# Padding mask tables of the last attention layer: built by ScalarE one phase earlier, and read by TensorE at a block address

## The chip, the cores and the metric

The kernel runs on one NeuronCore of a Trainium2 chip. A core has TensorE (matrix products), VectorE (DVE), ScalarE (ACT), GpSimd (POOL) and SyncE (SP, which issues the DMAs here), each with its own instruction stream, joined by semaphores. The metric is the device time of one execution in microseconds; the median of the executions counts.

## What is computed

The input x is 64 sequences of 64 tokens of width 256. Four transformer layers with a conditioning vector follow each other, each an attention and an MLP: layer 0 (one head, softmax then gelu MLP), layer 1 (16 heads of 16, rotary, gated MLP), layer 2 (16 heads of 64), layer 3 (16 heads of 16, with a padding mask). All is float32 in accuracy. What matters here is the mask of layer 3:

```python
attn = jnp.einsum('bhnd,bhmd->bhnm', q, k) * scale
mask = padding_mask[:, None, :] & padding_mask[:, :, None]
attn = jnp.where(mask[:, None, :, :], attn, -1000000000.0)
attn = jax.nn.softmax(attn, axis=-1)
```

## The kernel before

**Tiling.** The 4096 tokens are cut into 8 blocks of 512 (8 sequences, 4 tiles of 128 tokens). The work runs in 8 phases: attn 0, mlp 0, attn 1, mlp 1, attn 2, mlp 2, attn 3, mlp 3. In each phase the 8 blocks go through one body: block 0 is written out, blocks 1 to 6 are a hardware loop on each engine, block 7 is written out. `order_of` gives, by hand, the order of the stages in a body; every engine walks that same list and emits only its own part of each stage. `own`, `prev` and `nxt` are stages of this block, of the one before and of the one after: while a block's products run, the next one is normalised (`stats`, `norm`), transposed (`turn`), and split (`split`).

**Precision.** A float32 product is made of three products of a high and a low part (lines 541 to 543 of `project`). So every activation is split: ScalarE writes the high part (`h_hi`, line 766; `hid_hi`, line 896), VectorE subtracts it (`h_lo`, line 1030; `hid_lo`, line 1141). Those subtractions read two operands from SBUF. The weights of the next phase are split by GpSimd in eight shares, one to a block: stage `share`, `split_next`, a CAST (line 1187) and a subtraction (TENSOR_TENSOR, line 1189). SP loads the next share into `stage` when the one before it is split.

**The mlp body.** `up` k is a product of the block's 512 tokens with 128 hidden columns, into one of two score banks; ScalarE applies gelu (line 891) and the high part (line 896); VectorE makes `hid_lo`; `down` k accumulates. TensorE runs up 3, down 1, up 4, down 2, up 5, down 3, then `turn` (line 578, which transposes `xn`, the output of VectorE's `norm`, line 1010 in layers 0 and 1 and line 1012 in layers 2 and 3), up 6, down 4 and so on.

**GpSimd's part of it.** In `stats` GpSimd adds eps and takes the power (lines 1228, 1230). In block 0 of mlp 0 and of mlp 2 the stage `share` first calls `prepare_attention`, which clears the key and value tiles of the coming layer (memsets, lines 1194 to 1200). In mlp 2 it then calls `prepare_mask`: four TENSOR_SCALARs over 128x2048 (lines 1209, 1210) turn the uint8 `mask_rows` into two bf16 tables, `mask_qs` and `mask_ks`. Only then is the share of the weights split.

**The attn 3 body.** For each of 8 head groups (`scores` k), TensorE puts a mask product (line 629) into the bank before the score products (line 632). That product reads `mask_q_now` and `mask_k_now`, which hold the tiles of the current block only. The stage `mask` fills them: GpSimd copies four tiles of each table (line 1219), once for c = 0 and once for c = 1 of each block. The copy for c = 1 stands at the top of the body and waits until all scores of the block before are done (`s_full1`); the copy for c = 0 of the next block stands after `scores` 5. The stage `share` stands behind the first of them on GpSimd. In attn 1 and attn 3 GpSimd also adds the shift in `turn` (line 1235) into `hm`, from which ScalarE makes `h_hi` and VectorE `h_lo`. In VectorE's order, `scores` 4 and `back` (line 1164) stand ahead of `split` (line 1030).

Of the kernel before, what the change touches and what calls it, by code (L numbers as in the profile page):

```python
# [29 lines left out]
ALU = mybir.AluOpType  # L30
# [47 lines left out]
def order_of(kind, layer):  # L78
# [23 lines left out]
    if layer in (1, 3):  # L102
        mask = (lambda c, off: [("mask", c, off)]) if layer == 3 else (lambda c, off: [])
        return mask(1, 0) + [own("scores", 0), prev("probs_t", 7), own("q", 1), own("q_out", 1), prev("pv", 6), own("share"),
                own("scores", 1), own("probs_t", 0), own("v", 0), prev("pv", 7), own("v_out", 0), own("v", 1),
                own("v_out", 1), nxt("stats"),
                own("scores", 2), nxt("norm"), own("probs_t", 1), prev("merge"), own("k", 1), own("k_out", 1), own("pv", 0),
                own("scores", 3), own("probs_t", 2), prev("proj"), own("pv", 1), nxt("turn"),
                own("scores", 4), own("probs_t", 3), prev("back"), nxt("split"), own("pv", 2),
                own("scores", 5)] + mask(0, 1) + [own("probs_t", 4), own("pv", 3), nxt("k", 0), nxt("k_out", 0),  # L110
                own("scores", 6), own("probs_t", 5), own("pv", 4), nxt("q", 0), nxt("q_out", 0),
                own("scores", 7), own("pv", 5), own("probs_t", 6)]
# [38 lines left out]
def counts_of(kind, layer):  # L151

    c = dict(stats_raw=1, stats=1, mean_sq=1 if layer < 2 else 0, rstd_in=1, rstd=1, normed=1, eps_added=1, modded=2,
             h_hi=2, h=2, out_rows=2, x_done=1)
    if kind == "mlp":
        n = HID * (2 if layer == 1 else 1)
        c.update({"s_full0": n // 2, "s_full1": n // 2, "s_free0": n // 2, "s_free1": n // 2,
                  "hid32": HID, "hid_hi": HID, "hid": HID, "down": HID, "gate_in": HID if layer == 1 else 0,
                  "back": 1})
        return c  # L160
    n = 1 if layer == 0 else PAIRS
    c.update({"s_full0": n - n // 2, "s_full1": n // 2, "s_free0": n - n // 2, "s_free1": n // 2,
              "row_max": n, "shifted": n * (2 if layer == 0 else 1), "t_full": 0 if layer == 2 else n, "probs_t": n})
    if layer in (0, 2):
        c.update(probs=n, row_sum=n, row_inv=n, divided=n)
    if layer == 0:
        c.update(q=2, k=2, v=2, w_full=3, w_free=1, att_hi=2, att=2)
    if layer in (1, 3):
        c.update(o_full=n, o_inv=n // 2, o_free=n // 2, q=2 * 2, k=4 * 2, v=2 * 2, q32=2, w_full=3, w_free=1, att_hi=2, att=2)
    if layer == 1:  # L170
        c.update(rot_a=4, rot_b=4, k32=2)
    if layer == 3:
        c.update(mask_now=2)
    if layer == 2:
        c.update(q=n, k=n, v=8, o_full=n, o_free=n, att_hi=n, att=n, proj=n, w_full=1)
    return c
# [6 lines left out]
def build(nc, x_in, cond_in, mask_k_in, mask_q_in, vec_in, modw_in, weights_in, out, phases=len(PHASES)):  # L183
# [13 lines left out]
    with ExitStack() as ctx:  # L197
# [7 lines left out]
        w0_ready = ctx.enter_context(nc.semaphore("w0_ready"))  # L205
        t1_ready = ctx.enter_context(nc.semaphore("t1_ready"))
        mask_cleared = ctx.enter_context(nc.semaphore("mask_cleared"))
        mask_loaded = ctx.enter_context(nc.semaphore("mask_loaded"))
# [37 lines left out]
        eps_t = place("eps_t", [P, 4, TILES], F32)  # L246
        half_t = place("half_t", [P, TILES], F32)
        mx = place("mx", [P, 2, SEQ], F32)
        sm = place("sm", [P, 2, SEQ], F32)
# [34 lines left out]
        v0_sb = place("v0_sb", [P, TILES, D], F32, free + 12288)  # L284
        mask_q_now = place("mask_q_now", [P, 2, TILES, P], BF16, free3 + 4096)
        mask_k_now = place("mask_k_now", [P, 2, TILES, P], BF16, free3 + 6144)
        mask_qs = place("mask_qs", [P, tiles, 2, S], BF16, wb + 32768)
# [107 lines left out]
        def is_first(b):  # L395

            return isinstance(b, int) and b == 0
# [93 lines left out]
        def _(pe):  # L491
# [65 lines left out]
            def stage_of(ph, s, k, b):  # L557
# [42 lines left out]
                elif s == "scores":  # L600
# [23 lines left out]
                    else:  # L624
                        pe.wait_ge(sem["q"], n_at("q", ph, b, 2 * (c + 1)))
                        pe.wait_ge(sem["k"], n_at("k", ph, b, 4 * (c + 1)))
                        if layer == 3:
                            pe.wait_ge(sem["mask_now"], n_at("mask_now", ph, b, c + 1))
                            nc.tensor.matmul(dst.rearrange("p (r w) -> p r w", w=P), mask_q_now[:, c, j, :],
                                             mask_k_now[:, c, j, :].unsqueeze(1).to_broadcast([P, 4, P]), start=True, stop=False)  # L630
                        for g in range(2):
# [107 lines left out]
        def _(act):  # L739
# [7 lines left out]
            def table_part(n):  # L747
                if n == 0:
                    nc.scalar.activation(cond_silu[:, :, :], cond[:, :, :], ACT.Silu).then_inc(mod_act, 1)
                    act.wait_ge(mod_mm, 2)  # L750
                    for kc in range(DC):
                        nc.scalar.activation(t1_g[:, kc, :], psum[:, TABLE_BANKS[0], (2 + kc) * batch:(3 + kc) * batch],
                                             ACT.Silu, bias=col("t1_b", 2 + kc)).then_inc(mod_act, 1)

            def stage_of(ph, s, k, b):
                kind, layer = PHASES[ph]
                c, j, slot = k // 4, k % 4, k % 2
                if s == "table":
                    table_part(k)
                if is_first(b) and (s, k) == ("k_out", 0):  # L760
                    act.wait_ge(prepared, 4 if layer == 1 else 8)
# [146 lines left out]
        def _(dve):  # L908
# [21 lines left out]
            nc.vector.memset(half_t[:, :], -0.5).then_inc(consts_ready, 1)  # L930
            nc.vector.memset(pb[:, :, :], 0.0).then_inc(consts_ready, 1)
            full = 8 * batch
            dve.wait_ge(consts_ready, 6)
# [237 lines left out]
        def _(pool):  # L1171
# [32 lines left out]

            def prepare_mask():

                pool.wait_ge(mask_loaded, 16)
                for g in range(2):
                    nc.gpsimd.tensor_scalar(mask_qs[:, :, g, :], mask_rows[:, :, :], -MASKED, None, ALU.mult).then_inc(prepared, 1)
                    nc.gpsimd.tensor_scalar(mask_ks[:, :, g, :], mask_rows[:, :, :], 0.0, col("ident", g), ALU.is_equal, ALU.mult).then_inc(prepared, 1)  # L1210
                prepares[0] += 4
                pool.wait_ge(prepared, prepares[0])

            def mask_of_block(ph, c, b):

                pool.wait_ge(sem["s_full1"], n_at("s_full1", ph, b, -2 if c == 0 else 0))
                now = bass.ds(b * TILES, TILES)
                for dst, src in ((mask_q_now, mask_qs), (mask_k_now, mask_ks)):
                    ins = nc.gpsimd.tensor_copy(dst[:, c, :, :].rearrange("p t (g k) -> p t g k", k=S), src[:, now, :, :])
                ins.then_inc(sem["mask_now"], 1)  # L1220

            prepares = [0]
            def stage_of(ph, s, k, b):
# [19 lines left out]
                elif s == "divide":  # L1243
# [6 lines left out]
                    nc.gpsimd.tensor_tensor(ap, ap, inv, ALU.mult).then_inc(sem["divided"], 1)  # L1250
                elif s == "mask":
                    mask_of_block(ph, k, b)
                elif s == "share":
                    if is_first(b):
                        pool.wait_ge(sem["x_done"], n_at("x_done", ph, 0, 1))
                        if PHASES[ph + 1:ph + 2] in ([("attn", 1)], [("attn", 3)]):
                            prepare_attention()
                        if PHASES[ph + 1:ph + 2] == [("attn", 3)]:
                            prepare_mask()
                    split_next(ph, b)  # L1260
# [96 lines left out]
```

## Time and profile before

| | us |
|---|---|
| median of 3 runs | 2225.43 |
| lowest and highest | 2223.94 and 4509.24 |
| the profiled execution, whole | 2222.83 |
| its span from first to last instruction | 2221.0 |
| TensorE busy in that span | 2087.0 |
| VectorE busy | 1344.9 |
| ScalarE busy | 997.9 |
| GpSimd busy | 407.9 |

Busy times of different engines overlap. Of the three timed runs two lie 1.5 us apart and one stands far away.

### The profile page before, as it was taken

Reading aid. Unit: us, or ns where it says so; the run is one execution under the profiler, and the core shown is the slowest. Engines: PE = TensorE matmul, PEld = TensorE weight load, DVE = VectorE, ACT = ScalarE, POOL = GpSimd, SP = SyncE. Lnnn points to the kernel's source line nnn. Section 1 sums busy time; section 2 is a strip of 40 time slices with the busy share of each in tenths; the row PEclk is TensorE's granted clock in tenths of the full one; section 3 lists DMA queues with packets and bytes.
Section 4 is the critical chain, followed back from the end, with each engine's and each line's share of the span. In section 5 each row is a group of like instructions: output and inputs, shape, how many; then the busy total and the mean of one; then the engine's idle time right before and its main releaser. Section 6 shows DMA issues by size and latency. Waiting matters only on the chain.

```text
span 2221.0 us, 45198 instructions
## 1 busy us (share of the span) xinstructions
PE 2087.0 (94%) x15856; PEld 1692.9 (76%) x15856; DVE 1344.9 (61%) x2570; ACT 997.9 (45%) x1608; POOL 407.9 (18%) x425
## 2 busy tenths in 40 slices
PE   5889999999999999999999999998899999999998
PEld 4777788777777778787777777776688787787887
DVE  4564665667767565654555544546766677775664
ACT  2443455545444333334444444444344555554443
POOL 1121211223222010110112111112511222220000
PEclk9999999999999999999999999999999999999999
DMA  5000000000000000000000000000000000000000
GB/s 213 10 14 9 8 11 7 15 8 14 7 14 10 10 19 9 19 10 11 7 6 5 0 5 5 5 1 13 5 7 5 10 10 10 5 5 1 28 19 29
DMA packets 17855, 33.30 MB, mean 15 GB/s; under 512 B 1266, under 2 KB 11762, under 8 KB 17138
## 3 DMA queue, kind: packets, MB, share of 16 engines
q1 hardware_dynamic: 17778, 32.25, 4.5%
q8 instruction: 50, 0.82, 0.2%
q14 instruction: 27, 0.22, 0.0%
HBM read 28.06 MB, written 4.19 MB: 15 GB/s over the span
## 4 chain that ended last, share of the span: by engine, by line
PE 76%; DVE 10%; issue 8%; ACT 3%; POOL 2%; DVEq 0%; DMA 0%; ACTq 0%; SPq 0%; POOLq 0%
PE psum L541 20%; PE psum L543 19%; PE psum L542 19%; PE psum L632 4%; PE psum L645 3%; PE psum L578 2%; PE psum L665 2%; PE psum L731 2%; PE psum L679 1%; PE psum L621 1%; DVE xn L1010 1%; DVE h_lo L1030 1%; PE psum L498 1%; DVE hm L1020 1%; DVE hm L1025 1%
## 5 line engine op out<-in xcount | busy, mean ns | idle before, releaser
L541 PE MATMUL psum<-h_hi,w_lo 128*128 128x512 f32 x1152 | 479.7, 416 | 28.2 <-DVE h_lo L1030 21.6
L543 PE MATMUL psum<-h_hi,w_hi 128*128 128x512 f32 x1152 | 457.9, 398 | 0.0
L542 PE MATMUL psum<-h_lo,w_hi 128*128 128x512 f32 x1152 | 457.7, 397 | 0.0
L1141 DVE TENSOR_TENSOR hid_lo<-hid,hid_hi 128x512 fp32r<-128x512 f32 x256 | 201.7, 788 | 263.2 <-ACT hid_hi L896 262.9
L541 PEld LDWEIGHTS psum<-h_hi,w_lo 128*128 128x128 f32 x1152 | 218.8, 190 | 85.4 <-issue 25.8
L896 ACT ACTIVATE hid_hi<-hid 128x512 fp32r<-128x512 f32 x256 | 161.9, 632 | 225.7 <-PE psum L543 134.7
L543 PEld LDWEIGHTS psum<-h_hi,w_hi 128*128 128x128 f32 x1152 | 218.1, 189 | 53.8
L542 PEld LDWEIGHTS psum<-h_lo,w_hi 128*128 128x128 f32 x1152 | 218.7, 190 | 42.1
L1082 DVE TENSOR_REDUCE mx<-psum 128x8 f32<-128x512 f32 x192 | 132.4, 690 | 160.6 <-PE psum L621 107.3
L891 ACT ACTIVATE hid<-psum,vec 128x512 f32<-128x512 f32 x192 | 131.9, 687 | 199.9 <-PE psum L543 197.9
L541 PE MATMUL psum<-hid_hi,w_lo 128*128 128x512 f32 x512 | 202.8, 396 | 5.8 <-DVE hid_lo L1141 3.9
L542 PE MATMUL psum<-hid_lo,w_hi 128*128 128x512 f32 x512 | 201.1, 393 | 0.0
L543 PE MATMUL psum<-hid_hi,w_hi 128*128 128x512 f32 x512 | 200.3, 391 | 0.0
L1228 POOL TENSOR_TENSOR ms<-ms,eps_t 128x4 f32<-128x4 f32 x64 | 14.2, 222 | 895.6 <-DVE ms L1005 468.0
L1250 POOL TENSOR_TENSOR pb<-pb,ri 128x512 f32<-128x512 f32 x72 | 75.1, 1043 | 523.2 <-DVE ri L1097 523.2
L632 PE MATMUL psum<-kx,qb 128*128 128x256 f32 x512 | 136.5, 389 | 14.2 <-ACT qb L828 9.6
L645 PE MATMUL psum<-vec,pb 128*128 128x128 f32 x800 | 123.1, 277 | 24.0 <-ACTq L797 13.1
L645 PEld LDWEIGHTS psum<-vec,pb 128*128 128x128 f32 x800 | 96.8, 141 | 53.3 <-issue 24.6
L1085 DVE TENSOR_TENSOR pb<-psum,mx 128x512 f32<-128x512 f32 x192 | 132.8, 692 | 6.6
L541 PEld LDWEIGHTS psum<-hid_hi,w_lo 128*128 128x128 f32 x512 | 96.2, 188 | 30.5 <-DVE hid_lo L1141 4.9
L857 ACT ACTIVATE pt<-psum 128x512 f32<-128x512 f32 x128 | 76.2, 595 | 94.6 <-PE psum L645 89.6
L1164 DVE TENSOR_TENSOR xres<-xres,psum 128x1024 f32 (+1 forms) x64 | 78.1, 1221 | 66.6 <-PE psum L731 62.4
(118 smaller groups left out, 3717.3 us busy)
## 6 DMA issues: line engine op xcount, KB each, us to landing
stage<-in_w_dram SPq DMA_DIRECT2D x24, 256.0 KB, 2.7
stage<-in_w_dram SPq DMA_DIRECT2D x8, 512.0 KB, 3.5
out_dram<-xres SPq DMA_DIRECT2D x8, 512.0 KB, 2.9
xres<-in_x_dram SPq DMA_DIRECT2D x1, 3584.0 KB, 18.9
modw_mod<-in_modw_dram SPq DMA_DIRECT2D x2, 1536.0 KB, 13.8
stage<-in_w_dram SPq DMA_DIRECT2D x8, 384.0 KB, 3.3
stage<-in_w_dram SPq DMA_DIRECT2D x8, 192.0 KB, 2.4
modw_film<-in_modw_dram SPq DMA_DIRECT2D x1, 1024.0 KB, 6.9
```

The costliest lines, as they stand in the source:

```text
L541: nc.tensor.matmul(dst, s_lo, m_hi, start=start and j == 0, stop=False)
L542: nc.tensor.matmul(dst, s_hi, m_lo, start=False, stop=False)
L543: ins = nc.tensor.matmul(dst, s_hi, m_hi, start=False, stop=stop and j == len(pairs) - 1)
L632: ins = nc.tensor.matmul(dst.rearrange("p (r g k) -> p r g k", g=2, k=S)[:, :, g, :], qb[:, c, 2 * j + g, :, :].rearrange("p h q -> p (h q)"),
L645: ins = nc.tensor.transpose(dst[:, t * P:(t + 1) * P], pb[:, slot, t * P:(t + 1) * P], ident)
L857: nc.scalar.activation(pt[:, slot, :], probs_tp, ACT.Exp, scale=SCORE_SCALE[layer]).then_inc(sem["probs_t"], 1)
L891: nc.scalar.activation(hid32[:, slot, :], scores[slot], func, bias=col(f"u{layer}", k)).then_inc(sem["hid32"], 1)
L896: nc.scalar.activation(hid_hi[:, slot, :], hid32[:, slot, :], ACT.Copy).then_inc(sem["hid_hi"], 1)
L1082: nc.vector.tensor_reduce(top, sc, AX.X, ALU.max).then_inc(sem["row_max"], 1)
L1085: nc.vector.tensor_tensor(dst, sc, top, ALU.subtract).then_inc(sem["shifted"], 1)
L1141: nc.vector.tensor_tensor(hid_lo[:, slot, :], hid32[:, slot, :], hid_hi[:, slot, :].bitcast(F32), ALU.subtract).then_inc(sem["hid"], 1)
L1164: nc.vector.tensor_tensor(xs, xs, src, ALU.add).then_inc(sem["x_done"], 1)
```

## The change

The tables `mask_qs` and `mask_ks` are made by ScalarE. `mask_table(n)` is one ACTIVATE over 128x2048; n = 0 to 3 are issued in block 0 of mlp 2 ahead of the gelus of up 3, 4, 5 and 6. The signs of the two tables are both turned: `mask_qs` is +MASKED times the mask, and `mask_ks` is (mask times a one-hot column) minus that column, taken as the bias `no_seq`, which VectorE writes at the start of the kernel. `prepare_mask` on GpSimd is gone. The copies to `mask_q_now` and `mask_k_now`, the stage `mask`, its semaphore and TensorE's wait for it are gone. The mask product reads the tables at tile `b * TILES + j`: in the hardware loop this address comes from a register. TensorE waits once, ahead of the first mask product, for the finished tables.

```diff
 (order_of, layers 1 and 3)
-        mask = (lambda c, off: [("mask", c, off)]) if layer == 3 else (lambda c, off: [])
-        return mask(1, 0) + [own("scores", 0), prev("probs_t", 7), own("q", 1), own("q_out", 1), prev("pv", 6), own("share"),
+        return [own("scores", 0), prev("probs_t", 7), own("q", 1), own("q_out", 1), prev("pv", 6), own("share"),
...
-                own("scores", 5)] + mask(0, 1) + [own("probs_t", 4), own("pv", 3), nxt("k", 0), nxt("k_out", 0),
+                own("scores", 5), own("probs_t", 4), own("pv", 3), nxt("k", 0), nxt("k_out", 0),
 (TensorE, scores)
-                            pe.wait_ge(sem["mask_now"], n_at("mask_now", ph, b, c + 1))
-                            nc.tensor.matmul(dst.rearrange("p (r w) -> p r w", w=P), mask_q_now[:, c, j, :],
-                                             mask_k_now[:, c, j, :].unsqueeze(1).to_broadcast([P, 4, P]), start=True, stop=False)
+                            if k == 0 and is_first(b):
+                                pe.wait_ge(mask_made, 5)
+                            q_bad, k_bad = (m.rearrange("p t g k -> p t (g k)")[:, bass.ds(b * TILES + j, 1), :]
+                                            for m in (mask_qs, mask_ks))
+                            nc.tensor.matmul(dst.rearrange("p (r w) -> p r w", w=P), q_bad.rearrange("p t w -> p (t w)"),
+                                             k_bad.to_broadcast([P, 4, P]), start=True, stop=False)
 (ScalarE)
+            def mask_table(n):
+
+                g = n % 2
+                if n < 2:
+                    nc.scalar.activation(mask_qs[:, :, g, :], mask_rows[:, :, :], ACT.Copy, scale=MASKED).then_inc(mask_made, 1)
+                else:
+                    nc.scalar.activation(mask_ks[:, :, g, :], mask_rows[:, :, :], ACT.Identity, bias=no_seq[:, g:g + 1],
+                                         scale=col("ident", g)).then_inc(mask_made, 1)
+
...
+                if PHASES[ph] == ("mlp", 2) and s == "up" and 3 <= k < 7 and is_first(b):
+                    if k == 3:
+                        act.wait_ge(mask_loaded, 16)
+                        act.wait_ge(mask_made, 1)
+                        act.wait_ge(sem["x_done"], n_at("x_done", ph, 0, 1))
+                    mask_table(k - 3)
 (VectorE, start of the kernel)
+            nc.vector.tensor_scalar(no_seq[:, :], col("ident", 0, 2), -1.0, None, ALU.mult).then_inc(mask_made, 1)
 (GpSimd)
-            def prepare_mask():
-
-                pool.wait_ge(mask_loaded, 16)
-                for g in range(2):
-                    nc.gpsimd.tensor_scalar(mask_qs[:, :, g, :], mask_rows[:, :, :], -MASKED, None, ALU.mult).then_inc(prepared, 1)
-                    nc.gpsimd.tensor_scalar(mask_ks[:, :, g, :], mask_rows[:, :, :], 0.0, col("ident", g), ALU.is_equal, ALU.mult).then_inc(prepared, 1)
...
-            def mask_of_block(ph, c, b):
-
-                pool.wait_ge(sem["s_full1"], n_at("s_full1", ph, b, -2 if c == 0 else 0))
-                now = bass.ds(b * TILES, TILES)
-                for dst, src in ((mask_q_now, mask_qs), (mask_k_now, mask_ks)):
-                    ins = nc.gpsimd.tensor_copy(dst[:, c, :, :].rearrange("p t (g k) -> p t g k", k=S), src[:, now, :, :])
-                ins.then_inc(sem["mask_now"], 1)
...
-                        if PHASES[ph + 1:ph + 2] == [("attn", 3)]:
-                            prepare_mask()
```

## Rows read from the trace of the kernel before

**Rows 1.** The page: busy us by engine, and the chain's shares by engine.

```profile
PE 2087.0 (94%) x15856; PEld 1692.9 (76%) x15856; DVE 1344.9 (61%) x2570; ACT 997.9 (45%) x1608; POOL 407.9 (18%) x425
...
PE 76%; DVE 10%; issue 8%; ACT 3%; POOL 2%; DVEq 0%; DMA 0%; ACTq 0%; SPq 0%; POOLq 0%
```

**Rows 2.** Busy by window, stats to stats: block 0 of mlp 2, mlp 0, mlp 3.

```profile
core 0: us, PE busy (x) PEld busy (x) DVE busy (x) ACT busy (x) POOL busy (x), PEclk, DMA share, GB/s
1546.79:1585.92 39.13, 26.61 (x110) 21.25 (x109) 31.50 (x30) 11.06 (x17) 35.31 (x13) 0.87 0.01 4
223.99:252.47 28.48, 24.78 (x109) 20.13 (x109) 18.29 (x29) 12.20 (x20) 9.40 (x8) 0.94 0.02 7
2031.89:2055.03 23.14, 23.14 (x110) 18.94 (x109) 13.68 (x30) 10.98 (x17) 1.72 (x2) 1.00 0.01 1
```

**Rows 3.** Timeline of PE: start, us, what, [idle before <- releaser]; mlp 2, then mlp 0.

```profile
1560.21 1.97 PE L578 MATMUL psum<-vec,xn 128*128 128x128 f32 x8 [8.58 <-DVE xn L1012]
...
1572.16 0.50 PE L541 MATMUL psum<-hid_hi,w_lo 128*128 128x512 f32 x1 [3.93 <-DVE hid_lo L1141]
...
232.32 1.97 PE L578 MATMUL psum<-vec,xn 128*128 128x128 f32 x8 [3.70 <-DVE xn L1010]
```

**Rows 4.** Timeline of DVE, block 0 of mlp 2, then of mlp 0.

```profile
1548.63 11.52 DVE L1012 TENSOR_SCALAR xn<-xres,mv,rstd 128x256 f32<-128x256 f32 x4 [1.18 <-POOL rstd L1230]
...
1567.99 4.12 DVE L1141 TENSOR_TENSOR hid_lo<-hid,hid_hi 128x512 fp32r<-128x512 f32 x1
...
225.69 6.58 DVE L1010 TENSOR_SCALAR xn<-xres,rstd 128x256 f32<-128x256 f32 x4 [1.18 <-POOL rstd L1230]
232.19 2.08 DVE L1141 TENSOR_TENSOR hid_lo<-hid,hid_hi 128x512 fp32r<-128x512 f32 x2
```

**Rows 5.** Timeline of POOL, block 0 of mlp 2.

```profile
1548.54 3.52 POOL L1194 MEMSET kx<- 128x4096 f32 x1
...
1554.63 5.38 POOL L1209 TENSOR_SCALAR mask_qs<-mask_rows 128x2048 bf16<-128x2048 uint8 x1
...
1573.29 7.66 POOL L1210 TENSOR_SCALAR mask_ks<-mask_rows,vec 128x2048 bf16<-128x2048 uint8 x1
```

**Rows 6.** ACT: timeline in mlp 2, then groups by form (busy, mean ns).

```profile
1551.66 0.63 ACT L896 ACTIVATE hid_hi<-hid 128x512 fp32r<-128x512 f32 x1 [0.69 <-PE psum L543]
...
L896 ACT ACTIVATE hid_hi<-hid 128x512 fp32r<-128x512 f32 x256 | 161.9, 632 | 225.7 <-PE psum L543 134.7 <-DVE hid L1136 82.2
...
L836 ACT ACTIVATE pb<-pb 64x256 f32<-64x256 f32 x16 | 6.7, 416 | 17.4 <-DVE pb L1068 17.3
```

**Rows 7.** Timeline of POOL, one turn of attn 3's loop.

```profile
1864.99 2.04 POOL L1235 TENSOR_TENSOR hm<-hm,mod 128x512 f32<-128x512 f32 x2 [9.29 <-DVE hm L1020]
...
1876.79 0.61 POOL L1219 COPY mask_k_now<-mask_ks 128x512 bf16 x1
1877.35 0.61 POOL L1187 CAST w_hi<-stage 128x512 f32 x1
1878.13 1.28 POOL L1189 TENSOR_TENSOR w_lo<-stage,w_hi 128x512 f32 x1 [0.17 <-POOL w_hi L1187]
```

**Rows 8.** Timelines of DVE and PE, the same turn of the loop.

```profile
1868.18 1.29 DVE L1030 TENSOR_TENSOR h_lo<-hm,h_hi 128x512 fp32r<-128x512 f32 x2
...
1869.60 0.49 PE L541 MATMUL psum<-h_hi,w_lo 128*128 128x512 f32 x1 [0.91 <-DVE h_lo L1030]
```

**Rows 9.** Timelines of POOL and DVE, mlp 1: a weight split beside a two-input subtraction.

```profile
782.55 2.42 POOL L1189 TENSOR_TENSOR w_lo<-stage,w_hi 128x1024 f32 x1 [0.17 <-POOL w_hi L1187]
...
782.67 2.85 DVE L1141 TENSOR_TENSOR hid_lo<-hid,hid_hi 128x512 fp32r<-128x512 f32 x1 [0.70 <-ACT hid_hi L896]
```

**Rows 10.** Timeline of DVE, the last h_lo ahead of attn 3.

```profile
1741.59 1.98 DVE L1030 TENSOR_TENSOR h_lo<-hm,h_hi 128x512 fp32r<-128x512 f32 x2 [0.61 <-ACT h_hi L766]
```

**Rows 11.** Timeline of PE: first mask product of a loop block, then of block 7.

```profile
1877.55 0.39 PE L629 MATMUL psum<-mask_k_now,mask_q_now 128*128 128x512 bf16 x1 [0.30 <-POOL mask_k_now L1219]
...
1977.52 0.38 PE L629 MATMUL psum<-mask_k_now,mask_q_now 128*128 128x512 bf16 x1 [0.18 <-issue]
```

More of the change, by code:

```diff
@@ L171, in counts_of @@
         c.update(rot_a=4, rot_b=4, k32=2)
-    if layer == 3:
-        c.update(mask_now=2)
     if layer == 2:
@@ L206, in build @@
         t1_ready = ctx.enter_context(nc.semaphore("t1_ready"))
+        mask_made = ctx.enter_context(nc.semaphore("mask_made"))
         mask_cleared = ctx.enter_context(nc.semaphore("mask_cleared"))
@@ L247, in build @@
         half_t = place("half_t", [P, TILES], F32)
+        no_seq = place("no_seq", [P, 2], F32)
         mx = place("mx", [P, 2, SEQ], F32)
@@ L284, in build @@
         v0_sb = place("v0_sb", [P, TILES, D], F32, free + 12288)
-        mask_q_now = place("mask_q_now", [P, 2, TILES, P], BF16, free3 + 4096)
-        mask_k_now = place("mask_k_now", [P, 2, TILES, P], BF16, free3 + 6144)
         mask_qs = place("mask_qs", [P, tiles, 2, S], BF16, wb + 32768)
@@ L1203, in prepare_attention @@
                     pool.wait_ge(prepared, prepares[0])
-            def prepare_mask():
-                pool.wait_ge(mask_loaded, 16)
-                for g in range(2):
-                    nc.gpsimd.tensor_scalar(mask_qs[:, :, g, :], mask_rows[:, :, :], -MASKED, None, ALU.mult).then_inc(prepared, 1)
-                    nc.gpsimd.tensor_scalar(mask_ks[:, :, g, :], mask_rows[:, :, :], 0.0, col("ident", g), ALU.is_equal, ALU.mult).then_inc(prepared, 1)
-                prepares[0] += 4
-                pool.wait_ge(prepared, prepares[0])
-            def mask_of_block(ph, c, b):
-                pool.wait_ge(sem["s_full1"], n_at("s_full1", ph, b, -2 if c == 0 else 0))
-                now = bass.ds(b * TILES, TILES)
-                for dst, src in ((mask_q_now, mask_qs), (mask_k_now, mask_ks)):
-                    ins = nc.gpsimd.tensor_copy(dst[:, c, :, :].rearrange("p t (g k) -> p t g k", k=S), src[:, now, :, :])
-                ins.then_inc(sem["mask_now"], 1)
             prepares = [0]
@@ L1250, in stage_of @@
                     nc.gpsimd.tensor_tensor(ap, ap, inv, ALU.mult).then_inc(sem["divided"], 1)
-                elif s == "mask":
-                    mask_of_block(ph, k, b)
                 elif s == "share":
```

## The prediction

> **What bounds the kernel.** I read the page first. TensorE is busy 2087.0 of 2221.0 us and 76% of the chain that ended last is its matmuls [rows 1]. GpSimd is busy 18% of the span. So taking work off GpSimd is worth nothing by itself; it is worth something only where GpSimd makes someone late, and the sum has to be made from TensorE's idle time at the places that the change touches. Those are block 0 of mlp 2 and attn 3.
>
> Next I read the windows. From the `stats` of one block to the `stats` of the next, block 0 of mlp 2 takes 39.13 us. The same stretch of mlp 0 takes 28.48 and that of mlp 3 takes 23.14 [rows 2]. The three phases do the same number of matmuls (109 or 110) on blocks of one size. They differ in what GpSimd does: 35.31 us of work, 9.40 us, 1.72 us. mlp 3 prepares nothing, mlp 0 only clears tiles, mlp 2 clears tiles and builds the mask tables.
>
> The timeline of TensorE says where the 16 us over mlp 3 sit: it stands still 8.58 us for `xn` and 3.93 us for a `hid_lo` [rows 3]. Neither waits for GpSimd by name. But the timeline of VectorE shows the two producers stretched: four `norm` instructions take 11.52 us and one `hid_lo` 4.12 us [rows 4], while GpSimd runs without a pause from the memset at 1548.54 to the end of the last table at 1580.95 [rows 5]. In mlp 3's stretch, with 1.72 us of GpSimd, VectorE does the same list in 13.68 us instead of 31.50 [rows 2]. GpSimd's long instructions hold VectorE up, and VectorE holds TensorE up.
>
> A rule of the Trainium skill says why (SBUF — State Buffer, section Who interferes with whom): VectorE and GpSimd share one pair of SBUF ports, and a VectorE instruction in a two-port mode, or one with two SBUF inputs against a GpSimd instruction that reads SBUF, waits for the whole of the other's instruction. The stretched rows agree.
>
> **Part 1: the tables leave GpSimd in mlp 2.** Removed are four TENSOR_SCALARs, from 1554.63 to 1580.95, so 26.3 us of GpSimd [rows 5]. The memsets stay. Block 0 of mlp 0 is this case already played: the same memsets beside the same `norm`, then one share of weights. There `norm` takes 6.58 us, TensorE stands 3.70 us for it, and no second gap follows [rows 3, 4]. So I take the difference of the two windows: 39.13 - 28.48 = 10.65 us saved [rows 2]. A check by pieces: `norm` starts at 1548.63 and would end 6.58 later, at 1555.2, so `turn` starts there instead of at 1560.21, 5.0 us earlier [rows 3, 4]; the gap of 3.93 goes; together 8.9. The rest is clock: TensorE's mean granted clock in the window is 0.87 against 0.94 [rows 2]. Of 39.13 us, 13% below full is 5.1 us of lost clock, against 1.7 in mlp 0; part of that difference of 3.4 falls into idle time, the rest makes up the remaining 1.7. Both ways meet near 10.6.
>
> **Part 2: ScalarE makes them.** Four ACTIVATEs over 2048 elements. The trace has none so long. From 256 and 512 elements, 0.416 and 0.632 us, the slope is 0.84 ns an element, so one takes 0.632 + 1536 x 0.00084 = 1.93 us, an estimate; four are 7.7 us [rows 6]. ScalarE now stands idle about 0.7 us ahead of each gelu and again ahead of each high part, 1.4 us to a chunk of hidden columns [rows 6]. Three tables ahead of the high part of up 5 therefore make it 3 x (1.93 - 1.4) = 1.6 us late: it ends near 1553.9 instead of 1552.29 [rows 6]. Nobody notices: VectorE takes `hid_lo` 4 and 5 only after `norm`, that is after 1555.2, and the fourth table falls into TensorE's remaining wait of some 3.6 us. I book 0. If a table took twice as long, the high part of up 5 would be ready near 1559.6 and TensorE's down 5 would wait 1 to 2 us; that end goes into the range. `no_seq` is one tiny VectorE instruction while the input is loading: 0. TensorE's wait for the tables comes a whole phase after they are done: 0.
>
> **Part 3: the copies go from attn 3.** The copies themselves (0.61 us each, 32 of them [rows 7]) delay nothing in the loop: each set is copied well before the product that reads it, and in the loop's turn shown here `h_lo` takes its normal 1.29 [rows 8]. At the entry they do: they run beside the split of block 0's `h`, and that pair takes 1.98 us against 1.29 in the loop [rows 8, 10]. TensorE waits for it. Saved: 0.69 us, once.
>
> **Part 4: what moves into the hole.** `share` stood behind a copy that waited for the last scores of the block. So its CAST ran at 1877.35 and its subtraction at 1878.13 [rows 7], when VectorE was reading PSUM. Without that wait nothing holds it: the load of the share was issued when the one before it was split, most of a turn earlier, and GpSimd reaches it right after `turn`, whose two adds end at 1867.03 [rows 7]. CAST starts near 1866.97, the subtraction 0.78 later, at 1867.75, and it lasts 1.28 us, to 1869.03 [rows 7]. But at 1868.18 VectorE starts `h_lo`, the pair for which TensorE already waits 0.91 us in each block [rows 8]. mlp 1 shows this meeting: GpSimd's subtraction ends at 784.97 and VectorE's, started during it, at 785.52, 0.55 us behind [rows 9]. So the first `h_lo` ends at 1869.03 + 0.55 = 1869.58 and the second, 0.61 later, at 1870.19 instead of 1869.47: 0.72 us late. There is no slack, because TensorE is waiting for it, and all that follows in the block moves with it. This happens in the turns of blocks 1 to 7, seven times: 7 x 0.72 = 5.0 us lost. (For block 0's turn, where copies stretched `h_lo` too, I take the same: the subtraction is as much longer than the copy.)
>
> By the skill's rule taken literally (the same section: the whole instruction is held) `h_lo` would begin only at 1869.03 and take its full 0.69, so 0.86 late, seven times 6.0 us and a saving 1 us smaller than mine. The rule speaks against this half of the change, and agrees with the row of mlp 1 in kind.
>
> **Part 5: addresses from a register.** In the loop each mask product needs two addresses, and loses a wait. 48 products have them (8 in each of blocks 1 to 6). No matmul of the kernel before has a register address. Where the sequencer is ahead of the array this is free. At the top of the loop it is not: there the idle time before the product is 0.30 us, against 0.18 in block 7, where all values are constants [rows 11]. That difference of 0.12 pays for the few register steps with which the loop works out the values that it waits for, so two steps more and one less cost up to 0.1 us. Booked: 6 x 0.1 = 0.6. Lower end 0; upper end 0.2 at each of the 48, 9.6 us.
>
> **The sum.** -10.65 - 0.69 + 5.0 + 0.6 = -5.7 us. The span goes from 2221.0 to 2215.3, the profiled execution from 2222.83 to about 2217.1. The median of before is 2.6 above its profiled execution, so the median after is 2225.43 - 5.7 = 2219.7.
>
> **The rivals.**
> 1. *The weight split does not collide* (GpSimd reaches it later, or VectorE gets in first). For it: the two start only 0.43 us apart. Against it: their order follows from one event, VectorE's `hm`. Then parts 1, 3 and 5 stand alone: -10.7, time 2214.7.
> 2. *Slower: the register addresses are paid at every product.* The gain without them is 6.3 us; over 48 products it is gone from 0.13 us each on. With 0.2 us each it is +9.6 - 6.3 = +3.3, time 2228.7. Against it: in the loop only the first product of a block has such idle time before it.
> 3. *ScalarE is late*: a table takes far more than 1.9 us, or the function with a bias and a column scale reloads its table. Costs 2 to 3 us: 2222.
> 4. *mlp 0 is a poor model* and the gap for `xn` stays, since the memsets make it, or shrinks more than there. Plus or minus 2 us: 2218 to 2222, inside the forecast.
>
> **How the numbers follow.** Forecast with rival 4: 0.55. Rival 1: 0.22. Rival 2: 0.10. Rival 3: 0.10. Something unforeseen: 0.03. The likeliest case gives 2219.7, its own range 2217 to 2222. With rival 1 below and most of rival 2 above, and executions of this kernel 1.5 us apart, the range is 2212 to 2228. A measurement of this kernel tells 2% from no change, that is 44.5 us; the largest gain in these cases is 11 us. So: faster 0.01, same 0.97, slower 0.02.
>
> **What would show it.** Part 1: the window of mlp 2's block 0 near 28.5 us, `norm` near 6.5, one gap of about 3.6 and no gap for `hid_lo`. Part 2: four ACTIVATEs of 1.9 us. Part 3: `h_lo` at the entry of attn 3 at 1.3. Part 4: the CAST directly after line 1235's adds, `h_lo` pairs of 2.0 instead of 1.29 and TensorE's wait for them 1.6 instead of 0.91 in each block; the loop's turn 0.8 longer. Part 5: 0.4 instead of 0.30 before the first mask product, none before the others. I am wrong if the loop of attn 3 does not get longer (rival 1), or gets longer by more than 1.5 us a turn (rival 2).

## The result and the profile after

| | before | after |
|---|---|---|
| median, us | 2224.35 (6 executions) | 2204.87 (6 executions) |
| lowest and highest | 2222.47 and 4509.24 | 2200.37 and 2206.74 |
| the profiled execution, whole | 2222.83 | 2205.29 |
| its span | 2221.0 | 2203.5 |

The ratio is 0.991, with an interval of 0.9896 to 0.9923: 19.5 us faster, where 5.7 were forecast, and below the range (2212). By 2% it is the same. One execution of before took 4509.24 us; why isn't known, and the median is 2224.28 without it. The page of after, to be read against [rows 1]:

```profile
PE 2072.0 (94%) x15856; PEld 1698.5 (77%) x15856; DVE 1336.2 (61%) x2571; ACT 1003.3 (46%) x1612; POOL 361.5 (16%) x389
...
PE 77%; DVE 9%; issue 8%; ACT 3%; POOL 1%; DVEq 0%; DMA 0%; ACTq 0%; SPq 0%; POOLq 0%
```

TensorE issues the same 15856 products and is busy 15 us less. No part of my sum does that. Both spans, cut at the first `stats` of each phase, say where the time went:

| phase | before, us | after, us | difference |
|---|---|---|---|
| attn 0 | 177.28 | 177.40 | +0.1 |
| mlp 0 | 219.39 | 216.43 | -3.0 |
| attn 1 | 304.36 | 308.00 | +3.6 |
| mlp 1 | 293.79 | 291.04 | -2.8 |
| attn 2 | 508.19 | 504.25 | -3.9 |
| mlp 2 | 227.04 | 214.01 | -13.0 |
| attn 3 | 257.65 | 263.37 | +5.7 |
| mlp 3 | 233.30 | 229.00 | -4.3 |

The change touches mlp 2 and attn 3: together -7.3. The other 10 us come from phases in which no instruction was changed. The mlp loops and that of attn 2 are shorter there. Windows of five loop blocks of mlp 0 and five of mlp 2 (columns as in [rows 2]), of before:

```profile
252.47:372.63 120.16, 120.16 (x561) 98.39 (x560) 71.81 (x146) 63.92 (x101) 16.09 (x20) 1.00 0.03 8
```

```profile
1609.88:1730.05 120.17, 120.17 (x562) 98.39 (x561) 76.83 (x151) 57.84 (x90) 14.45 (x21) 1.00 0.02 6
```

and of after:

```profile
252.32:370.23 117.91, 117.91 (x562) 98.33 (x561) 71.78 (x146) 63.57 (x101) 16.11 (x20) 1.00 0.03 8
...
1593.18:1711.13 117.95, 117.95 (x562) 98.35 (x561) 76.40 (x151) 57.67 (x90) 14.42 (x20) 1.00 0.02 6
```

Same number of products, no idle time, granted clock 1.00 in all four, and 2.2 us less: 24.03 us a block became 23.59. The groups of TensorE by line within the windows of mlp 2 show which products. Of before:

```profile
L543 PE MATMUL psum<-h_hi,w_hi 128*128 128x512 f32 x80 | 31.6, 395 | 0.0
L543 PE MATMUL psum<-hid_hi,w_hi 128*128 128x512 f32 x81 | 31.6, 390 | 0.0
L542 PE MATMUL psum<-h_lo,w_hi 128*128 128x512 f32 x80 | 31.6, 395 | 0.0
L541 PE MATMUL psum<-hid_hi,w_lo 128*128 128x512 f32 x80 | 31.5, 394 | 0.0
```

and of after:

```profile
L540 PE MATMUL psum<-hid_hi,w_hi 128*128 128x512 f32 x81 | 31.6, 390 | 0.0
L540 PE MATMUL psum<-h_hi,w_hi 128*128 128x512 f32 x80 | 31.2, 390 | 0.0
L538 PE MATMUL psum<-hid_hi,w_lo 128*128 128x512 f32 x80 | 31.2, 390 | 0.0
L539 PE MATMUL psum<-h_lo,w_hi 128*128 128x512 f32 x80 | 31.1, 389 | 0.0
```

Products that took 394 to 395 ns now take 390, as those that already did. The durations overlap; the distance from one product's start to the next is what counts. In before its median in these blocks is 234 to 235 ns for the products of `up` and 231 to 232 for those of `down`; in after it is 227 for both. A block of the loops of mlp 0, 2 and 3 is 24.03 - 23.58 = 0.45 us shorter, one of attn 2 too (63.96 to 63.51), one of mlp 1 0.49 (35.81 to 35.32). If blocks 0 and 7 gain as much, this is 8 x (4 x 0.45 + 0.49) = 18.3 us. Attn 0 adds 8 x 0.04, and attn 1 8 x 0.14 (38.90 to 38.76, in turns at full clock): 19.7 in all, an estimate.

Now the places that the prediction spoke of. Block 0 of mlp 2, window and then the timelines of TensorE, VectorE and GpSimd (against [rows 2 to 5]):

```profile
1541.96:1569.83 27.87, 24.62 (x111) 20.40 (x110) 19.44 (x30) 16.91 (x22) 8.68 (x8) 0.94 0.02 5
```

```profile
1549.85 1.97 PE L575 MATMUL psum<-vec,xn 128*128 128x128 f32 x8 [3.25 <-DVE xn L1028]
```

```profile
1543.28 6.52 DVE L1028 TENSOR_SCALAR xn<-xres,mv,rstd 128x256 f32<-128x256 f32 x4 [0.30 <-POOL rstd L1229]
1549.72 1.81 DVE L1157 TENSOR_TENSOR hid_lo<-hid,hid_hi 128x512 fp32r<-128x512 f32 x2
```

```profile
1543.19 3.53 POOL L1210 MEMSET kx<- 128x4096 f32 x1
1546.65 1.93 POOL L1211 MEMSET vb<- 128x2176 f32 x1
```

The stretch fell from 39.13 to 27.87; one gap of 3.25 us is left and the one for `hid_lo` is gone. The first of the four `norm` instructions alone lasts from 1543.28 to 1548.73, through both memsets; two of the other three take 0.40 us. ScalarE in the same place, with the last two of the four tables (the first two take 1.89 us each):

```profile
1545.26 2.08 ACT L761 ACTIVATE mask_ks<-mask_rows,no_seq,vec 128x2048 bf16<-128x2048 uint8 x1
1547.25 0.67 ACT L906 ACTIVATE hid<-psum,vec 128x512 f32<-128x512 f32 x1
1548.03 0.63 ACT L911 ACTIVATE hid_hi<-hid 128x512 fp32r<-128x512 f32 x1
1548.57 2.08 ACT L761 ACTIVATE mask_ks<-mask_rows,no_seq,vec 128x2048 bf16<-128x2048 uint8 x1
```

One turn of attn 3's loop, GpSimd, VectorE, TensorE (against [rows 7, 8]):

```profile
1848.94 2.05 POOL L1234 TENSOR_TENSOR hm<-hm,mod 128x512 f32<-128x512 f32 x2 [9.32 <-DVE hm L1036]
1850.93 0.61 POOL L1203 CAST w_hi<-stage 128x512 f32 x1
1851.71 1.27 POOL L1205 TENSOR_TENSOR w_lo<-stage,w_hi 128x512 f32 x1 [0.17 <-POOL w_hi L1203]
```

```profile
1852.14 1.99 DVE L1046 TENSOR_TENSOR h_lo<-hm,h_hi 128x512 fp32r<-128x512 f32 x2
```

```profile
1854.27 0.49 PE L538 MATMUL psum<-h_hi,w_lo 128*128 128x512 f32 x1 [1.62 <-DVE h_lo L1046]
...
1862.23 0.39 PE L629 MATMUL psum<-mask_ks,mask_qs 128*128 x1 [0.34 <-ACT qb L843]
```

The share of the weights moved into the hole and met `h_lo`, as forecast: 1.99 us instead of 1.29, and TensorE waits 1.62 instead of 0.91. The loop's turn went from 33.37 to 34.10 us.

### The profile page after: what moved, and what is told of

It is laid out like the page before. It is cut to its first block, busy times and chain, and to the rows that moved or that the text cites. A ratio compares the mean times of both kernels' runs of the same rounds, so it can differ in the third digit from the quotient of the medians.

```text
span 2203.5 us, 45089 instructions
## 1 busy us (share of the span) xinstructions
PE 2072.0 (94%) x15856; PEld 1698.5 (77%) x15856; DVE 1336.2 (61%) x2571; ACT 1003.3 (46%) x1612; POOL 361.5 (16%) x389
## 4 chain that ended last, share of the span: by engine, by line
PE 77%; DVE 9%; issue 8%; ACT 3%; POOL 1%; DVEq 0%; DMA 0%; ACTq 0%; SPq 0%; POOLq 0%
PE psum L538 21%; PE psum L540 19%; PE psum L539 19%; PE psum L632 4%; PE psum L645 3%; PE psum L575 2%; PE psum L665 2%; PE psum L731 2%; PE psum L679 1%; PE psum L618 1%; DVE h_lo L1046 1%; DVE xn L1026 1%; PE psum L495 1%; DVE pb L1101 1%; DVE hm L1041 1%
## 5 line engine op out<-in xcount | busy, mean ns | idle before, releaser
L1157 DVE TENSOR_TENSOR hid_lo<-hid,hid_hi 128x512 fp32r<-128x512 f32 x256 | 193.9, 758 | 255.6 <-ACT hid_hi L911 255.6
L1227 POOL TENSOR_TENSOR ms<-ms,eps_t 128x4 f32<-128x4 f32 x64 | 13.6, 212 | 978.2 <-DVE ms L1021 555.7
L645 PE MATMUL psum<-vec,pb 128*128 128x128 f32 x800 | 124.3, 279 | 24.3 <-ACTq L812 13.3
L632 PEld LDWEIGHTS psum<-kx,qb 128*128 128x128 f32 x512 | 95.6, 194 | 29.3 <-issue 15.4
```

Of the source, the lines that this page charges most:

```text
L632: ins = nc.tensor.matmul(dst.rearrange("p (r g k) -> p r g k", g=2, k=S)[:, :, g, :], qb[:, c, 2 * j + g, :, :].rearrange("p h q -> p (h q)"),
L645: ins = nc.tensor.transpose(dst[:, t * P:(t + 1) * P], pb[:, slot, t * P:(t + 1) * P], ident)
L1157: nc.vector.tensor_tensor(hid_lo[:, slot, :], hid32[:, slot, :], hid_hi[:, slot, :].bitcast(F32), ALU.subtract).then_inc(sem["hid"], 1)
```

## The question left, and the theories

The forecast parts are all there, yet another 14 us went. The change has one thing that costs no time and that I did not weigh: a tile. `no_seq` is 8 bytes a partition, takes a slot of 32, and `place`, which gives each tile the next free address, puts it in front of `mx` and all that follows. The weights, `hid_hi`, `hid_lo`, `at_hi`, `at_lo`, `kx` and the rest begin 32 bytes later than before; `xn`, `hm`, `h_hi`, `h_lo` and `stage` stay. In before the latter begin 32 bytes past a multiple of 64 and the weights and `hid` at a multiple of 64; in after all begin at 32 past.

**Theory A**: the new place of the tiles brings TensorE's products closer together. Its rival, **B**: the changed work itself does it, or it is no effect of the kernel at all. Once A stood, two forms of it were told apart: **C**, what counts is where the operands stand against each other modulo 64 bytes, and **D**, it is good for the weights and `hid` to stand at 32.

## The experiments

**e1_pad32: the shift alone.** The kernel before, with an unused tile where the change has `no_seq`.

```diff
         half_t = place("half_t", [P, TILES], F32)
+        place("pad", [P, 8], F32)
         mx = place("mx", [P, 2, SEQ], F32)
```

> The kernel before with one unused tile of 32 bytes placed where the change puts no_seq, and nothing else: no instruction differs, only the addresses of every tile behind it. Theory A (the new tile's 32 bytes moved the weights against the activations, and that makes the split products faster): an mlp block goes from 24.03 to 23.6 us, the spacing of the products from about 234 to 227 ns, the whole kernel is 7 to 10 us faster than before, block 0 of mlp 2 keeps its two gaps and the loop of attn 3 keeps 33.4 us or a little less. Theory B (the faster products come from the instructions that left GpSimd, or from the chip): an mlp block stays at 24.03 and the time is that of before.

Measured: 2208.72 us (2208.20 to 2216.38), ratio 0.9928 [0.9908, 0.9947]: 16.4 us faster than its neighbours of before (2225.12), with not one instruction changed, and more than the 7 to 10 expected. Windows: block 0 of mlp 2, five loop blocks of mlp 2, four of attn 3.

```profile
1546.82:1586.63 39.81, 27.35 (x110) 22.10 (x109) 31.44 (x30) 11.06 (x17) 34.97 (x13) 0.79 0.02 4
1610.15:1728.13 117.98, 117.98 (x562) 98.39 (x561) 76.43 (x151) 57.66 (x90) 14.45 (x21) 1.00 0.02 6
1852.22:1985.57 133.35, 128.62 (x1138) 105.69 (x1137) 98.53 (x193) 70.91 (x112) 29.56 (x40) 1.00 0.02 6
```

The loop blocks are those of after (117.98 for five), block 0 of mlp 2 and the turns of attn 3 (33.3) are those of before. Theory A is shown, B falls.

**e2_no_shift: the change alone.** The kernel after, with `no_seq` put behind the weights, so that no other tile moves.

```diff
-        no_seq = place("no_seq", [P, 2], F32)
...
         free3 = wa + 8 * 2048
+        no_seq = place("no_seq", [P, 2], F32, wb + 49152)
```

> The changed kernel with no_seq placed in the free bytes above all other tiles, so that every other tile has its address of before. Theory A: mlp blocks at 24.03 us again, and the change proper is left: block 0 of mlp 2 near 28.5 us, loop turns of attn 3 near 34.1 us, 5 to 7 us faster than before in all. Theory B: the time of the changed kernel, 19 us faster.

Measured: 2218.0 us (2215.9 to 2218.75, 9 executions), ratio 0.9966 [0.9953, 0.9979]: 7.1 us faster. The same three windows as for e1:

```profile
1548.81:1575.46 26.65, 23.60 (x111) 19.07 (x110) 19.42 (x30) 16.85 (x22) 8.68 (x8) 1.00 0.02 6
1599.26:1719.41 120.15, 120.15 (x562) 98.37 (x561) 76.84 (x151) 57.82 (x90) 14.45 (x20) 1.00 0.02 6
1846.88:1982.93 136.05, 128.52 (x1139) 105.46 (x1138) 101.20 (x193) 70.86 (x112) 20.33 (x25) 1.00 0.02 6
```

Loop blocks at 24.03 again, block 0 of mlp 2 at 26.65, attn 3's turn at 136.05 / 4 = 34.0. What the sum spoke of is worth 7.1 us, where it said 5.7.

**e3_tables: the tables alone.** The kernel before, with `mask_table` on ScalarE and `no_seq` high; the copies to `mask_q_now` and `mask_k_now` stay, with the old products, and the share stays behind them. The first copy waits for the tables.

```diff
 (ScalarE: mask_table and its call as in the change)
+        no_seq = place("no_seq", [P, 2], F32, wb + 49152)
 (GpSimd)
-                        if PHASES[ph + 1:ph + 2] == [("attn", 3)]:
-                            prepare_mask()
...
                 elif s == "mask":
+                    copies[0] += 1
+                    if copies[0] == 1:
+                        pool.wait_ge(mask_made, 5)
                     mask_of_block(ph, k, b)
```

> The kernel before with the tables made by ScalarE (no_seq in the free bytes above all tiles, no address moved), the copies and the place of the weight share in attn 3 kept. My steps 1 and 2 alone: block 0 of mlp 2 at about 28.3 us instead of 39.13, attn 3 as before with turns of 33.37 us, 10.5 to 11.5 us faster than before. If ScalarE's four tables cost something, less than that.

Measured: 2212.43 us (2210.01 to 2220.4), ratio 0.9942 [0.9921, 0.9963]: 12.7 us faster. Block 0 of mlp 2, and four turns of attn 3:

```profile
1557.97:1586.21 28.24, 25.18 (x111) 20.24 (x110) 19.44 (x30) 16.87 (x22) 8.69 (x8) 0.94 0.01 5
...
1854.48:1987.72 133.24, 128.53 (x1139) 105.47 (x1138) 98.49 (x193) 70.92 (x112) 29.55 (x40) 1.00 0.02 6
```

Part 1 alone is worth 39.13 - 28.24 = 10.9 us by the window, 12.7 by the medians. And e2 is 5.6 us slower than e3: the change is better without its second half.

**e4_held: the share kept away from `h_lo`.** The kernel after; in attn 3 GpSimd waits with the share until the block's scores are done, where the copies had held it before.

```diff
+                    if PHASES[ph] == ("attn", 3):
+                        pool.wait_ge(sem["s_full1"], n_at("s_full1", ph, b, 0))
                     split_next(ph, b)
```

> The changed kernel with one wait more: in attn 3 GpSimd takes the weight share only when the scores of the block before are done, which is when the copies let it go before. Theory of the collision: h_lo pairs back at 1.29 us, TensorE's wait ahead of the k product from 1.62 back to 0.91 us, loop turns 0.7 us shorter, the kernel 4.5 to 5.5 us faster than the changed one (about 2199.5). If the longer wait comes from something else in attn 3, the same time as the changed kernel.

Measured: 2202.0 us (2191.26 to 2205.7), ratio 0.9904 [0.9880, 0.9928]. Five turns of attn 3's loop:

```profile
1795.22:1962.01 166.79, 160.71 (x1422) 132.08 (x1421) 123.18 (x241) 88.63 (x140) 25.76 (x30) 1.00 0.02 6
```

166.79 / 5 = 33.36, the turn of before. So the 0.7 us a turn are the meeting of the share and `h_lo`, and the register addresses, which this kernel still has, cost about 0.03 a turn. The medians (2.9 us between e4 and after, four executions that differ by 14) don't resolve the 5 us that seven turns should give; the rows do.

**e5_all64, e6_weights32, e7_pad64, e9_both0: which place counts.** All are the kernel before with unused tiles.

```diff
 (e5)   + place("pad", [P, 8], F32) ahead of xn
 (e6)   + place("pad", [P, 8], F32) behind gate_in
 (e7)   + place("pad", [P, 16], F32) behind half_t
 (e9)   + place("pad", [P, 8], F32) ahead of xn, and another behind half_t
```

> The kernel before with 32 unused bytes ahead of xn, so that every tile from there on, the activations' high and low parts and the weights alike, moves by 32. The activations h_hi and h_lo, which lay 32 past a multiple of 64, then lie on one, the weights 32 past one, except where a tile keeps its place. Theory C (what counts is that both operands of a product lie alike against 64 bytes): nothing changes against the kernel before, 24.03 us an mlp block, since their distance is the same. Theory D (what counts is that the weights and hid tiles lie 32 bytes past a multiple of 64): the same gain as with the padding tile, 23.58 us an mlp block and 12 us or more in all.

> The kernel before with 32 unused bytes behind gate_in: only the weights and what shares their space move; hid_hi, hid_lo, pb and pt stay. Theory C (distance of the two operands): the up products (h against weights) become fast, about 227 ns apart, and the down products (hid against weights) get slower than their 231 ns; an mlp block stays between 23.6 and 24.1. Theory D (place of the weights alone): both fast, 23.58.

> The kernel before with 64 unused bytes at the place of no_seq: all tiles behind move, but keep their place against a multiple of 64. If the place against 64 bytes counts, nothing changes: 24.03 us an mlp block and the time of before. If any move of the addresses, or a place against 128 bytes, makes the difference, an mlp block comes out otherwise.

> The kernel before with two 32-byte paddings: one ahead of xn, one behind half_t. h_hi, h_lo, xn, hm and stage then begin at multiples of 64 bytes; the weights and hid_hi, hid_lo and all behind them move by 64 in all and begin at multiples of 64 as before. So the two operands of every product stand at the same place modulo 64, as in e1, but at 0 instead of 32. Theory C (what counts is the place of one operand against the other modulo 64): the product spacing of up falls as in e1, mlp blocks 23.6 us, time about 2209. Theory D (32 modulo 64 is good in itself): up products and down products then both have nothing at 32, so nothing is gained or something is lost: mlp blocks 24.0 or more, time 2224 or more.

Starts of tiles modulo 64, the median distance from one product's start to the next in a loop block of mlp 2, and the block:

| kernel | `h` | weights | `hid` | up, ns | down, ns | block, us | median, us |
|---|---|---|---|---|---|---|---|
| before | 32 | 0 | 0 | 235, 234 | 232, 231 | 24.03 | 2221 to 2225 |
| e7 | 32 | 0 | 0 | 235, 232 | 231, 231 | 23.97 | 2221.48 |
| e5 | 0 | 32 | 32 | 235, 231 | 233, 230 | 24.05 | 2225.46 |
| e6 | 32 | 32 | 0 | 230, 231 | 235, 234 | 24.00 | 2241.0 |
| e1, after | 32 | 32 | 32 | 227 | 227 | 23.58 | 2208.72, 2204.87 |
| e9 | 0 | 0 | 0 | 226 | 226 | 23.60 | 2207.53 |

(The two numbers are the distances after the first and after the second of the three products, medians over the loop of mlp 2.) The windows of e5, e6 and e9, five loop blocks of mlp 2 in each:

```profile
1611.32:1731.55 120.23, 120.23 (x562) 98.39 (x561) 76.79 (x151) 57.78 (x90) 14.44 (x21) 1.00 0.02 6
```

```profile
1604.79:1724.79 120.00, 120.00 (x562) 98.43 (x561) 76.79 (x151) 57.67 (x90) 14.45 (x21) 1.00 0.02 6
```

```profile
1600.17:1718.20 118.03, 118.03 (x562) 98.40 (x561) 76.43 (x151) 57.67 (x90) 14.46 (x21) 1.00 0.02 6
```

e5 has the weights and `hid` where after has them and gains nothing (ratio 1.0 [0.999, 1.001]): D falls. e9 has them where before has them and gains all of it (0.9931 [0.9904, 0.9957]), because `h` moved to them: C stands against D. e6 moves the weights to `h` and away from `hid`: up falls to 230 and down rises to 235, so the place against the weights counts, though the block keeps its 24.00 us. e7 moves by a whole 64 and changes next to nothing (0.9989 [0.9979, 0.9999], 0.06 us a block).

Three things C doesn't settle. A pair that stands alike takes 227 only where the other pair does too, and 230 to 233 otherwise. A product's weights are loaded while the one before it runs (98.39 of 120.17 us in the windows above), which may be why. But in e1, after and e9 `h` and `hid` also stand alike with each other, and in none of the slow kernels do they; no run has them alike and the weights elsewhere, so it isn't shown that the weights are needed for the gain. Second, in the fast kernels the weights begin a multiple of 512 bytes behind `h`, in the slow ones 32 more or less, or `hid` is off; a difference of 64 was not tried, so 64 may be 128 or more. Third, only the mlp loops come down to 227. A turn of attn 3 takes 33.36 us in e1 against 33.37, the products of `h` in attn 2 come down only to 232 and 230, and in attn 1 the products of `at_hi`, which stands alike with its weights in both kernels, go from 227 to 236 after the first. Why isn't known.

e6 is a miss in its time, ratio 1.0078 [1.0067, 1.009]: its profiled execution took 2217.46 us at a mean granted clock of 0.991, its other eight 2237.13 to 2245.15, at 0.984 to 0.988. Time x (1 - clock), an estimate of what the lower clock cost, is 20 us in the first and 31 in the mean of the others, so about 11 of the 24 us are clock. Two more traces were taken of it.

> The same kernel as e6 (32 bytes of padding behind gate_in), for a second trace. Its eight timed executions took 2237 to 2245 us at a mean granted clock of 0.984 to 0.988, its profiled one 2217.5 at 0.991. If this trace is of the long kind (about 2240), the extra 23 us must show as stretches at half the clock, 1.5 us lost in each, so some 15 more than the 11 of the first trace, with the loop blocks of mlp 0, 2 and 3 still at 24.0 us. If it is of the short kind (about 2217), the question stays open.

> The same kernel once more, for a third trace: the same two outcomes as in the run before.

They took 2221.88 and 2227.63 us, neither of them as long as the eight. What makes e6's long executions isn't known. One difference between the three traces was found: in the second and the third, one turn of attn 2 (the loop's second) takes 71.1 and 71.5 us instead of 63.6. The same turn is long in the profiled executions of e1 and e3 (70.9 and 72.1). TensorE in e1:

```profile
1144.91 1.13 PE L622 MATMUL psum<-k_sb,q_sb 64*64 64x64 f32 x32 [3.85 <-issue]
1147.68 1.14 PE L680 MATMUL psum<-pt,v_sb 64*64 64x64 f32 x32 [1.63 <-issue]
```

Two gaps that wait for nothing in the profile, 5.5 us, and a stretch at half the clock that begins in the first of them. It would account for the profiled executions of e1 and e3 (2216.38 and 2220.4) standing 7 to 10 us above their others, of which no trace exists. What makes the gaps is open.

**e8_late_clear: a version from what was learnt.** The kernel after, the share of attn 3 held as in e4, and `prepare_attention` moved out of block 0's `share` in mlp 0 and mlp 2 to behind the next block's `norm`: the memsets then run when VectorE is not in `norm`.

```diff
+                elif s == "turn" and PHASES[ph] in (("mlp", 0), ("mlp", 2)):
+                    if isinstance(b, int) and b == 1:
+                        pool.wait_ge(sem["normed"], n_at("normed", ph, b, 1))
+                        prepare_attention()
...
                     if is_first(b):
                         pool.wait_ge(sem["x_done"], n_at("x_done", ph, 0, 1))
-                        if PHASES[ph + 1:ph + 2] in ([("attn", 1)], [("attn", 3)]):
-                            prepare_attention()
+                    if PHASES[ph] == ("attn", 3):
+                        pool.wait_ge(sem["s_full1"], n_at("s_full1", ph, b, 0))
                     split_next(ph, b)
```

> The changed kernel with the held weight share of attn 3, and with GpSimd's memsets of the key and value tiles moved in mlp 0 and mlp 2 from ahead of the next block's norm to behind it. If the memsets are what stretches norm to 6.5 us, norm comes back to about 2 us, TensorE's wait for xn (3.70 and 3.25 us) goes, block 0 of mlp 0 and of mlp 2 takes about 23.8 us instead of 28.2 and 27.9, and the kernel is about 8 us faster than the one with the held share alone (2202.0), so about 2194. If the weight share then takes the memsets' place in the way of norm, half of that.

Measured: 2184.1 us (2181.0 to 2185.43), ratio 0.982 [0.9803, 0.9836]. It is 40 us below before, 21 below after, and 10 below the 2194 expected. Block 0 of mlp 0 and of mlp 2, then VectorE and GpSimd in the latter:

```profile
222.11:244.80 22.69, 22.69 (x110) 18.94 (x109) 13.21 (x29) 12.24 (x20) 8.87 (x8) 1.00 0.03 9
1531.17:1554.19 23.02, 23.02 (x111) 19.07 (x110) 14.40 (x30) 16.69 (x22) 8.11 (x8) 1.00 0.02 6
```

```profile
1532.49 1.93 DVE L1028 TENSOR_SCALAR xn<-xres,mv,rstd 128x256 f32<-128x256 f32 x4 [0.30 <-POOL rstd L1229]
```

```profile
1532.41 0.40 POOL L1203 CAST w_hi<-stage 128x256 fp32r<-128x256 f32 x1
1532.88 0.74 POOL L1205 TENSOR_TENSOR w_lo<-stage,w_hi 128x256 fp32r<-128x256 f32 x1
1534.48 3.53 POOL L1210 MEMSET kx<- 128x4096 f32 x1 [0.86 <-DVE xn L1028]
```

GpSimd does nearly the same work (8.1 us in that window, 8.7 in after), but the four `norm` instructions take 1.93 us instead of 6.52 (11.52 in before), TensorE never stands still, and its clock is 1.00 throughout. The short instructions of the share now run beside `norm` and cost it little: with nothing beside it, in block 0 of mlp 3 of before, it takes 1.38. This is the same cause as part 1 and about as large again: 28.23 - 22.69 = 5.5 us in mlp 0 and 27.87 - 23.02 = 4.9 in mlp 2, against after. Of the 21 us the held share is another 5.1. The remaining 5 were not located; the mean granted clock was higher too, 0.992 to 0.996 in e8's four executions, 0.988 to 0.992 in after's six.

## Why the prediction was right and wrong

**The step that failed** is the sentence in part 2: "`no_seq` is one tiny VectorE instruction while the input is loading: 0." It priced the instruction and not the tile. The place of the tile moves everything that is allocated behind it, and that is worth 16.4 us alone (e1) and 13.1 on top of the change (e2 to after; 12.4 with each set against its own neighbours), more than the whole rest. No row of before gives its price: before has both kinds of pair, `h` off its weights and `hid` on them, and they differ by only 3 ns, where the gain turned out to be 4 to 8 on both. But that a new tile in the middle of the allocation moves others could be read in the diff, and "something unforeseen", 0.03, was too little with that in view.

**Part 1** (-10.65): right. The window measured 27.87 in after, of which 0.45 is the shift, and 28.24 in e3, against 28.48 forecast; mlp 0 was the right model, down to its `norm` (6.52 against 6.58) and the single gap (3.25 against 3.6 forecast). In e2 it came out at 26.65, with a clock of 1.00 instead of 0.94: the last 1.5 us are whether a stretch at half the clock falls into the block. The rule quoted there, of the Trainium skill (SBUF — State Buffer, section Who interferes with whom), agrees with these rows: in after the first `norm` instruction ends only 0.15 us behind the second memset, and in e8, with the memsets out of its way, `norm` takes 1.93 us for four.

**Part 2** (0): right for ScalarE. The tables take 1.89 and 2.08 us, 1.93 was estimated. The high part of up 5 ends at 1548.66 and `norm` at 1549.80, so nobody waited.

**Part 3** (-0.69): right. Ahead of attn 3 `h_lo` takes 1.29 instead of 1.98 [rows 10], and TensorE's gap before its first product there went from 1.46 to 0.81.

**Part 4** (+5.0): right in place, mechanism and size. Seven turns at 34.10 - 33.37 = 0.73 are 5.1; e3 against e2 gives 5.6; e4 takes it away. The literal reading of the Trainium skill's rule in that part gave 0.86 a turn, 6.0 in all; the traces stand at 0.73, nearer to the row of mlp 1 [rows 9].

**Part 5** (+0.6): right, and smaller. The idle time before a loop block's first mask product went from 0.30 to 0.34 us, 0.2 us over six blocks. Rival 2 asked for 0.13 us at each of 48 products and is refuted. Rival 1 (no meeting) and rival 3 (ScalarE late) are refuted too.

**The sum** of the foreseen parts, -5.7, measured -7.1 in e2 (in its trace mlp 2 is 12.7 us shorter and attn 3 5.9 longer). The range was wrong because it was built from the foreseen parts only; its lower end was rival 1, another reading of part 4, and left no room for a term that had been put at 0.

**What the rows and the medians leave open.** The shorter distance between products is worth some 19.7 us by the loops, and medians gave 16.4 (e1), 13.6 (e9) and 13.1 (e2 to after). The rest comes back as stretches at half the clock (below): after's profiled execution has five between 529 and 730 us, before's has one. The mean granted clock of every execution is on record. Time x (1 - clock), an estimate of what the lower clock cost, is in the mean 24.3 us for e1 against 21.7 for its neighbours of before (without one of 2322.51 us), 23.2 for e9 against 18.1, and 22.0 for after against 16.3 for e2. Added to the medians' differences, these 2.6, 5.1 and 5.7 us make 19.0, 18.7 and 18.8. So the clock closes the sum to 1 us, and it was lower with the closer products in all three comparisons; what makes it lower is open.

## What to carry to other kernels

A new tile is an edit of every tile allocated behind it: hold the places of the others fixed when a change is to be measured, and try an unused tile of 32 bytes as an experiment of its own. An instruction that leaves an engine is worth what it did to its neighbour, and the hole it leaves is filled by what stood behind it: look whom that meets. If a long instruction cannot go, move it to where the neighbour isn't held by it (the memsets in e8, 10.4 us over two blocks).

## What the runs showed of the hardware

**Places of a product's two operands.** With float32 operands of 128x512 back to back in the mlp loops, the distance is 226 to 227 ns where the moving operands `h` and `hid` and the weights all start alike modulo 64 bytes (e1, e9), and 231 to 235 for a pair that differs by 32 (before, e5, e6, e7). The Trainium skill (SBUF — State Buffer, section Who interferes with whom) says that TensorE never waits on another engine and reads the two operands through independent ports; no run here tests the first, and the second doesn't mean that the operands' places don't matter: in e1 and e9 they are worth up to 8 ns a product and 2% of a turn of the mlp loops. Whether the reads themselves meet isn't shown.

**A long GpSimd instruction beside VectorE's `norm`.** Four `norm` instructions of 128x256 take 1.38 us with GpSimd idle (before, mlp 3), 1.93 beside a CAST and a subtraction of 1.1 us together (e8), 6.52 beside two memsets (after) and 11.52 beside the memsets and the first table (before):

```profile
2033.73 1.38 DVE L1012 TENSOR_SCALAR xn<-xres,mv,rstd 128x256 f32<-128x256 f32 x4 [1.18 <-POOL rstd L1230]
```

**Stretches at half the clock.** In each of the thirteen traces one to four appear in attn 1, of 3.4 us each, at a place that changes from one execution to the next. Windows of one turn of attn 1 in before, without and with one:

```profile
505.01:543.91 38.90, 36.79 (x302) 30.10 (x301) 27.73 (x54) 18.09 (x30) 10.95 (x10) 1.00 0.03 9
582.81:623.30 40.49, 38.39 (x302) 31.33 (x301) 27.73 (x54) 18.09 (x30) 10.96 (x11) 0.96 0.04 10
```

The mean granted clock is 0.96 instead of 1.00, TensorE fell from 2.4 to 1.2 GHz for part of the turn, and the turn is 1.6 us longer. Between 529 and 730 us before and after differ by four of them with the same instructions, so that a difference of 5 us between two medians of few executions says little here, and the windows say more.
